# Cross-attention and a gated low-rank layer on one core: another order on TensorE, transfers of 64 partitions, wider matmuls for the sums of squares

## The reference

```python
x = x + _L0_xattn_ref(_layernorm(x), ctx, ctx)     # x, ctx: (8, 512, 2048) float32
x = x + _L0_ffn_ref(_layernorm(x), router_w, A, B)

def _L0_xattn_ref(q, k, v):                # B, C, N = 8, 512, 2048; 8 heads of 64 channels
    qh = softmax(q over the 64 channels of a head)
    kh = softmax(k over the 2048 positions)
    kvs = einsum('bnhd,bnhe->bhde', kh, vh)
    out = einsum('bnhd,bhde->bnhe', qh, kvs)

def _L0_ffn_ref(x, router_w, A, B):        # 4 experts of rank 16, the best 2 are used
    logits = flat @ router_w.T
    gates = softmax(logits where among the top 2, else -inf)
    mid = einsum('tf,erf->ter', flat, A)
    delta = einsum('te,teo->to', gates, einsum('ter,eor->teo', mid, B) * 4.0)
```

## Time and profile before

| | |
|---|---|
| median of 3 runs | 493.88 us (493.44 to 500.45) |
| the profiled execution | 496.45 us, of it 494.7 us from the first to the last instruction (the span) |
| PE busy | 416.6 us (84%) |
| DVE busy | 378.6 us (77%) |
| POOL busy | 358.8 us (73%) |
| ACT busy | 300.2 us (61%) |
| granted TensorE clock, mean | 0.92 |
| DMA | 137.99 MB, mean 279 GB/s |

### The profile page before, as it was taken

One profiled execution on the slowest core, in us unless ns is written; L12 is line 12 of the kernel. 1 busy time (PEld: TensorE's weight loads), 2 busy tenths in 40 slices (PEclk: granted clock), 3 DMA queues, 4 the chain that ended last, 5 costly groups with the idle time before them and its releaser, 6 DMA issues.

```text
span 494.7 us, 22911 instructions
## 1 busy us (share of the span) xinstructions
PE 416.6 (84%) x9960; PEld 362.5 (73%) x9960; DVE 378.6 (77%) x1045; ACT 300.2 (61%) x404; POOL 358.8 (73%) x341
## 2 busy tenths in 40 slices
PE   6659888988978887887988896898897878999975
PEld 6648777877867676776877675787776767788864
DVE  2488758896868967887897876868895978976864
ACT  1367767766648566574867665666674848586410
POOL 0459978987869767877797876867895987898510
PEclk9657978999989988999899997988998999999997
DMA  8997877899899888999899997899997998755347
GB/s 300 416 366 219 295 225 258 257 298 326 260 315 291 237 315 277 288 315 299 298 280 350 294 303 248 251 310 301 336 302 227 326 296 284 247 177 207 121 187 256
DMA packets 38996, 137.99 MB, mean 279 GB/s; under 512 B 4208, under 2 KB 6384, under 8 KB 38768
## 3 DMA queue, kind: packets, MB, share of 16 engines
q1 hardware_dynamic: 38896, 136.52, 82.3%
HBM read 102.95 MB, written 33.55 MB: 276 GB/s over the span
## 4 chain that ended last, share of the span: by engine, by line
PE 72%; issue 12%; DVE 7%; DMA 4%; SPq 3%; POOL 1%; ACT 1%; DVEq 0%; POOLq 0%
PE num_ps L404 17%; PE kv_ps L384 15%; PE raw_ps L421 13%; PE delta_ps L469 10%; PE kv_ps L436 7%; PE delta_ps L470 6%; DMA ctx_sb<-in_ctxt_dram 4%; DVE y_sb L705 2%; DVE attnT L696 2%; PE kv_ps L369 2%; SPq L234 1%; PE raw_ps L455 1%; PE num_ps L361 1%; DVE bn_parts L638 1%; SPq L229 1%
## 5 line engine op out<-in xcount | busy, mean ns | idle before, releaser
L322 POOL TENSOR_TENSOR y_sb<-attnT,y_sb 128x512 f32<-128x512 f32 x128 | 164.2, 1283 | 68.1 <-DVE attnT L696 67.4
L310 POOL TENSOR_TENSOR ek_sb<-ctx_sb,kmax_row 128x512 f32<-128x512 f32 x128 | 167.4, 1309 | 41.5 <-ACT kmax_row L502 40.8
L705 DVE TENSOR_TENSOR y_sb<-delta_ps,y_sb 128x512 f32<-128x512 f32 x128 | 87.4, 685 | 55.9 <-PE delta_ps L470 54.9
L404 PE MATMUL num_ps<-kv_sb,x_sb 64*64 64x65 f32 x4096 | 97.3, 233 | 18.4 <-issue 11.8
L384 PE MATMUL kv_ps<-ctx_sb,ek_sb 128*64 128x65 f32 x2048 | 100.3, 241 | 14.3 <-issue 14.0
L404 PEld LDWEIGHTS num_ps<-kv_sb,x_sb 64*64 64x64 f32 x4096 | 78.1, 142 | 34.2 <-issue 20.3
L384 PEld LDWEIGHTS kv_ps<-ctx_sb,ek_sb 128*64 128x64 f32 x2048 | 79.6, 146 | 28.4 <-issue 17.8
L421 PE MATMUL raw_ps<-w_sb,y_sb 128*64 128x69 f32 x2048 | 93.5, 232 | 6.8 <-issue 6.8
L621 DVE TENSOR_REDUCE max_n<-ctx_sb 128x32 f32<-128x512 f32 x128 | 86.4, 677 | 11.1 <-DMA ctx_sb<-in_ctxt_dram 11.1
L696 DVE TENSOR_TENSOR attnT<-num_ps,rden 128x512 f32<-128x512 f32 x128 | 88.5, 691 | 4.5
L469 PE MATMUL delta_ps<-midT,b_hi 128*128 128x256 f32 x256 | 84.2, 349 | 3.8 <-issue 3.1
(11 more groups left out here) (62 smaller groups left out, 423.6 us busy)
## 6 DMA issues: line engine op xcount, KB each, us to landing
ctx_sb<-in_ctxt_dram SPq DMA_DIRECT2D x64, 520.0 KB, 5.5
x_sb<-in_x_dram SPq DMA_DIRECT2D x64, 512.0 KB, 6.3
y_sb<-in_xt_dram SPq DMA_DIRECT2D x64, 512.0 KB, 6.5
out_dram<-y_sb SPq DMA_DIRECT2D x60, 512.0 KB, 6.0
out_dram<-y_sb SPq DMA_DIRECT2D x8, 256.0 KB, 3.6
sq_a<-in_bt_dram SPq DMA_DIRECT2D x1, 1024.0 KB, 15.8
w_sb<-in_wt_dram SPq DMA_DIRECT2D x1, 552.0 KB, 9.5
cst<-in_consts_dram SPq DMA_DIRECT2D x1, 145.0 KB, 2.4
```

The lines of the kernel that those rows point to most:

```text
L310: pool.tensor_tensor(ek_sb[:, t % 2, chunks(g), :].rearrange("p (a b) c -> p a b c", b=2), ctx_sb[:, t % 4, 2 * g:2 * g + 2, 1:P + 1, :].r ...
L322: pool.tensor_tensor(y, attnT[:, g, :], y, ALU.add).then_inc(x1_made, 1)
L404: mm = pe.matmul(num_ps[n, h, j * (DH + 1):(j + 1) * (DH + 1)], x_sb[d, t % 4, c * P + half * DH:c * P + (half + 1) * DH], kv_sb[d, t % 2, ...
L705: dve.tensor_tensor(y, delta_ps[i % 2][:].rearrange("p (j t c) -> p t j c", j=2, t=2), y, ALU.add).then_inc(out_made, 1)
```

## The change

TensorE keeps its operations but runs them in two orders. In even quarters: delta, turn_max, sum_squares, fold_squares, numerator, kv, project. In odd quarters: project, kv, spread_kmax, numerator, turn_mid, delta. DVE adds a delta one quarter later (`add_delta(*delta_at(q - 1))`).

The core of the diff:

```diff
-            STEP = 4 // PIECES
-            for q in range(0, 4 * NT + 28, STEP):
...
+            ctx_piece = x_piece = xt_piece = out_piece = (cst_landed, 16)
+            for q in range(0, 4 * NT + 28):
+                part = q % 2
+                p, r = divmod(q - part - 26, 8)
                 if 0 <= p < NP - 1:
...
+                    t, k = 2 * p + r // 2 % 2, r // 4
+                    sp.wait_ge(out_made, 8 * p + 4 * (k + 1))
+                    after(sp, *out_piece)
+                    store(t, k, part)
+                    out_piece = (out_stored[t % 8], 64 * (t // 8) + 32 * k + 16 * part + 16)
+                t, r = divmod(q - part + 10, 4)
                 if 3 <= t < NT:
-                    after(sp, num_done, 4 * (t - 4) + r + STEP)
-                    load_x(t, r // STEP)
+                    after(sp, num_done, 4 * (t - 4) + r + 2)
+                    after(sp, num_done, quarters_done(q, 5))
+                    after(sp, *x_piece)
+                    load_x(t, r // 2, part)
...
-                t, r = divmod(q + 16, 4)
-                if t < NT:
-                    sp.wait_ge(kv_done, 4 * (t - 4) + r + STEP)
-                    load_ctx(t, r // STEP)
+                t, r = divmod(q - part + 14, 4)
+                if 4 <= t < NT:
+                    sp.wait_ge(kv_done, 4 * (t - 4) + r + 2)
+                    after(sp, kv_done, quarters_done(q, 0))
+                    after(sp, *ctx_piece)
+                    load_ctx(t, r // 2, part)
...
-                for k in range(NCH // 4):
-                    for s in range(4):
-                        sq = sq_b if k >= 2 else sq_a[:, t % 2, :]
-                        at = (4 * k + s) % 8 * P
-                        mm = pe.matmul(kv_ps[(t + 1) % 2][32 * s:32 * s + 32, 2 * P:3 * P], ones[:, 0:32],
-                                       sq[:, at:at + P], start=(k == 0), stop=(k == 3), skip_group_check=True)
+                to = kv_ps[(t + 1) % 2]
+                for s in range(4):
+                    sq = sq_b[:] if s >= 2 else sq_a[:, t % 2, :]
+                    at = s % 2 * 3 * P
+                    pe.matmul(to[32 * s:32 * s + 32, P:4 * P], ones[:, 0:32], sq[:, at:at + 3 * P],
+                              start=True, stop=False, skip_group_check=True)
+                for s in range(4):
+                    sq = sq_b[:] if s >= 2 else sq_a[:, t % 2, :]
+                    at = (6 + s % 2) * P
+                    mm = pe.matmul(to[32 * s:32 * s + 32, P:2 * P], ones[:, 0:32], sq[:, at:at + P],
+                                   start=False, stop=True, skip_group_check=True)
...
-                pe.matmul(raw_ps[p % 2][:, odd, COL_SQ:COL_SQ + 2], sq_sum[:, t % 2, :], ones[:, 0:2],
-                          start=False, stop=True, skip_group_check=True).then_inc(sq_done, 1)
+                for k in range(3):
+                    mm = pe.matmul(raw_ps[p % 2][:, odd, COL_SQ:COL_SQ + 2], sq_sum[:, t % 2, k, :], ones[:, 0:2],
+                                   start=False, stop=(k == 2), skip_group_check=True)
+                mm.then_inc(sq_done, 1)
...
             for q in range(FIRST, LAST + 1):
-                delta(*delta_at(q))
-                turn_max(q)
-                sum_squares(q)
-                if q == 1:
-                    sum_w()
-                numerator(*tile_at(q, 5))
-                spread_kmax(q)
-                kv(*tile_at(q, 0))
-                project(*tile_at(q, 7))
-                fold_squares(q)
-                turn_mid(q)
+                if q % 2 == 0:
+                    delta(*delta_at(q))
+                    turn_max(q)
+                    sum_squares(q)
+                    fold_squares(q)
+                    numerator(*tile_at(q, 5))
+                    kv(*tile_at(q, 0))
+                    project(*tile_at(q, 7))
+                else:
+                    project(*tile_at(q, 7))
+                    kv(*tile_at(q, 0))
+                    spread_kmax(q)
+                    numerator(*tile_at(q, 5))
+                    turn_mid(q)
+                    if q == 1:
+                        sum_w()
+                    delta(*delta_at(q))
```

More of the change, by code:

```diff
@@ L221, in _, with rows, load_ctx, load_x @@
         def _(sp):
[L222 to L227, removed]
+            XW = N // 2
+            CP = NCH // 4
+            YC = NCH // 2
+            def rows(part):
+                return slice(part * DH, (part + 1) * DH)
+            def load_ctx(t, k, part):
                 c = slice(k * CP, (k + 1) * CP)
-                sp.dma_start(ctx_sb[:, t % 4, c, :, :].rearrange("p a c b -> p a (c b)"),
-                             ctxt[t][:, c, :, :].rearrange("p a c b -> p a (c b)")).then_inc(ctx_landed[t % 4], 16)
-            def load_x(t, k):
+                sp.dma_start(ctx_sb[rows(part), t % 4, c, :, :].rearrange("p a c b -> p a (c b)"),
+                             ctxt[t][rows(part), c, :, :].rearrange("p a c b -> p a (c b)")
+                             ).then_inc(ctx_landed[t % 4], 16)
+            def load_x(t, k, part):
                 c = slice(k * XW, (k + 1) * XW)
-                sp.dma_start(x_sb[:, t % 4, c], x_rows[t * P:(t + 1) * P, c]).then_inc(x_landed[t % 4], 16)
-            def load_y(t, k):
+                sp.dma_start(x_sb[rows(part), t % 4, c], x_rows[t * P + part * DH:t * P + (part + 1) * DH, c]
+                             ).then_inc(x_landed[t % 4], 16)
+            def load_y(t, k, part):
                 c = slice(k * YC, (k + 1) * YC)
-                sp.dma_start(y_sb[:, t % 8, c, :], xt[t][:, c, :]).then_inc(y_landed[t % 8], 16)
-            def store(t, k):
+                sp.dma_start(y_sb[rows(part), t % 8, c, :], xt[t][rows(part), c, :]).then_inc(y_landed[t % 8], 16)
+            def store(t, k, part):
                 c = slice(k * YC, (k + 1) * YC)
-                sp.dma_start(out[t, :, c, :].rearrange("p j c -> p (j c)"),
-                             y_sb[:, t % 8, c, :].rearrange("p j c -> p (j c)")).then_inc(out_stored[t % 8], 16)
+                sp.dma_start(out[t, rows(part), c, :].rearrange("p j c -> p (j c)"),
+                             y_sb[rows(part), t % 8, c, :].rearrange("p j c -> p (j c)")
+                             ).then_inc(out_stored[t % 8], 16)
             def store_last(i):
@@ L251, in whole @@
             def whole(load, t):
-                for k in range(PIECES):
-                    load(t, k)
+                for k in range(2):
+                    for part in range(2):
+                        load(t, k, part)
             def quarters_done(q, offset):
@@ L285, in _ @@
                 if 2 <= t < NT:
[L286 removed]
                     if t >= 8:
[L288 to L293 removed]
+                        sp.wait_ge(out_stored[t % 8], 64 * (t // 8))
+                    after(sp, *xt_piece)
@@ new lines, in _ @@
+                    load_y(t, r // 2, part)
+                    xt_piece = (y_landed[t % 8], 64 * (t // 8) + 16 * r + 16 * part + 16)
+                t, r = divmod(q - part + 14, 4)
[4 more added lines that the diff above has]
+                    load_ctx(t, r // 2, part)
+                    ctx_piece = (ctx_landed[t % 4], 64 * (t // 4) + 16 * r + 16 * part + 16)
@@ L559, in copy_squares @@
                 after(act, sq_done, t - 1)
-                act.activation(sq_sum[:, t % 2, :], kv_ps[(t + 1) % 2][:, 2 * P:3 * P], ACT.Copy,
+                act.activation(sq_sum[:, t % 2, :, :].rearrange("p k c -> p (k c)"), kv_ps[(t + 1) % 2][:, P:4 * P], ACT.Copy,
                                scale=1.0 / 32.0).then_inc(sq_summed, 1)
@@ L816, in _ @@
                 bn_part(*tile_at(q, -5))
[L817 removed]
+                add_delta(*delta_at(q - 1))
                 if a is not None:
```

22 lines of the change are left out of this document (8 added, 14 removed).

## The result

The changed kernel took 675.6 us (median of 4, 673.92 to 679.71) against 494.04 us: 1.370 times as long, 95% interval 1.364 to 1.376. I had forecast 464 us with a range of 447 to 530. A ratio with an interval rests on the faster executions of both kernels alone, since single executions of the kernel before spread from 484 to 507 us, and so it can differ by 1 or 2% from the quotient of the medians.

What follows compares the result with a forecast made beforehand. TensorE was taken as the bound, with late instruction fetches. Terms of -33 - 10 - 13 - 3 + 13 = -46 us gave 3.06 us a quarter; the transfer pace of 3.2 replaced it: 60.2 + 112 x 3.2 + 43 = 462, forecast 464, range 447 to 530.

Steps and rivals of the forecast that it cites:

- Step 1: PE's waits for late instruction fetches: fewer bytes in flight remove two thirds of them, -33 us.
- Step 2: TensorE's clock: two thirds of the time lost at the lower clock is won back, -10 us.
- Step 3: Deltas on TensorE: two side by side take 1.14 instead of 1.34 us, -13 us.
- step 7: Numerators at unequal distances: two deltas cover the division while DVE is on time; if late, PE waits; no size.
- Steps 4 and 5: Squares on TensorE: the fold saves starts, -3 us; sum_squares takes two more matmuls a tile, +13 us.
- Step 6: Fold ahead of the numerator on PE: it waits for ACT's squares, +10 us, parallel to the transfer pace.
- Step 8: Pace of transfers: a quarter can't be shorter than one 256 KB landing, taken as 3.1 us, 3.2 with issue.
- rival C: Slower: the landing of transfers becomes the bound; 519 us at 3.7 us a quarter; chance 0.19.
- rival D: Much slower: transfers of 64 partitions don't get the full rate; 550 to 710 us; chance 0.14.

Runs made afterwards that it cites:

- e8: Changed kernel with two pieces of each kind in flight instead of one, each half with its own semaphores: 575.93 us.
- e4: Kernel before with only the squares of the change (three chunks per matmul in fold_squares and sum_squares): 486.16 us, 0.982 of before.
- e12: Kernel before with the change's squares and 256 KB pieces by quarter columns over 128 partitions, no landing wait: 497.68 us, 1.016 of before.
- e11: Kernel before with both the new TensorE order and the squares of the change, transfers unchanged: 501.23 us, 1.008 of before.
- e7: Changed kernel with pieces of 128 partitions by a quarter of the columns and without the landing waits: 498.07 us.
- e3: Kernel before with only TensorE's opposite order in odd quarters and DVE's addition one quarter later: 501.63 us, 1.023 of before.
- e5: All computation left out, SP alone moves data in eleven stages: 403 GB/s for loads over 128 partitions, 206 GB/s over 64.
- e2: Changed kernel with its 256 KB pieces cut by columns over 128 partitions, still one of each kind in flight: 618.11 us, 1.247 of before.
- e1: Kernel before with each 512 KB piece sent as two transfers of 64 partitions back to back, no landing wait: 538.08 us against 496.39.
- e6: Changed kernel without the four waits for the piece before of the same kind, pieces of 64 partitions kept: 577.83 us.

## Why the prediction was wrong, point by point

**What bounds the kernel before: right in the main.** "Issue" is late instructions: in the trace of the kernel before all 32 such idle times of PE over 0.5 us end 1.2 to 1.6 us after a packet of the instruction queue has ended, and in e8 all 31 do so 1.2 to 1.7 us after one, while such packets are 5 to 7 us apart in the median. That data in flight make them late is borne out by e8 against the change, the same computation and bytes, differing in the number of pieces in flight. Of PE from 100 to 500 us (e8):

```profile
PE num_ps L425 <- issue: 27.2, 12, 4.8
PE kv_ps L405 <- issue: 13.5, 6, 3.7
PE delta_ps L497 <- DVE y_sb L742: 10.5, 17, 1.6
```

and of the changed kernel from 100 to 600 us:

```profile
PE delta_ps L490 <- DVE y_sb L732: 58.2, 12, 5.9
PE kv_ps L383 <- DVE kmax L658: 41.2, 12, 4.5
...
PE raw_ps L435 <- issue: 1.8, 1, 1.8
```

Over the whole span it is 62.9 against 4.0 us. The two differ in one thing more: PE waits 145.9 us for DVE in the changed kernel and 46.0 in e8, and in such a wait a late fetch goes unseen, so not all of the 59 us need be shorter fetches. The rule of the Trainium skill that such crossings are mostly hidden ("Runtime: NRT & Kernel Launch", section "Instruction fetch mechanics") agrees with the changed kernel (4.0 us), not with the one before (49.8 us).

**Step 1, fetch stalls: right in direction.** Nearly all went, not two thirds, but in a kernel in which PE was no longer the bound, so it was worth nothing and the size stays unproven. Where PE still leads the chain, pieces of half the bytes took issue waits from 37.7 (e4) to 20.5 us (e12), and in the new order only from 37.4 (e11) to 34.5 (e7).

**Step 2, clock: wrong sign.** The issue waits went, and longer waits for data came: a mean granted clock of 0.92 became 0.776.

**Step 3, deltas side by side: the size right, the value wrong.** In the changed kernel two deltas take 308.51 to 309.66 us, 1.15 us as worked out:

```profile
308.51 0.39 PE L490 MATMUL delta_ps<-midT,b_hi 128*128 128x256 f32 x1
...
309.66 0.52 PE L450 MATMUL kv_ps<-sq_a,cst 128*32 128x384 f32 x2
```

But with PE as the bound (e3) the order gains nothing. I had the reason in step 7, DVE late, and gave it no price.

**Steps 4 and 5: sizes right within 0.08 us, the sum's sign wrong.** +10 us was forecast, e4 measured -1.8%; why is open.

**Step 6: right.** The fold waits 7.4 us for ACT in e3, where 10 were put.

**Step 8, the pace: this is the step that failed.** I saw the mechanism, a quarter not shorter than one landing, and bounded the landing at 2.8 to 4.2 us, then took 3.1 because "the rule itself holds back the traffic"; it measured 4.2 to 4.6. The rule does not hold traffic back here: when landings set the pace, nearly four pieces are always in flight, since each kind issues 0.1 us after its landing. The value for three others in flight belonged there, 4.0 to 4.2 us at 128 partitions (e5, e2), which is my upper bound. I also wrote that a piece of 256 KB was not in the trace. One was, in the page of the kernel before:

```profile
out_dram<-y_sb SPq DMA_DIRECT2D x8, 256.0 KB, 3.6
```

These are the last stores, over 128 partitions, issued some 0.9 us apart, so with about four in flight. With their 3.6 us the sum is 519 us, which is rival C and no longer "no change or faster". With 4.2 us, and 0.1 us to issue, my own sum gives 60 + 112 x 4.3 + 43 + 2, about 587 us; e2, the case for it, took 618, with 4.38 us a quarter and an end 15 us longer than I had. The rest is the half rate of 64 partitions, which lifts the landing to 4.2 to 4.6 us here and costs at the start (+17 us, in e1 and e6 as well). I had left it as rival D with 0.14, and its range of 550 to 710 us holds the result; that is partly luck, as it put on the partitions alone what the wait does for the larger part. e2 and e6 put 120 us on the wait and 80 on the partitions when each comes alone.

The miss adds up: the first 112 steps took 4.61 us and not 3.2, +158 us; the last 15 took 3.46 and not 2.85, +9; the start +17, the end +28. 464 and these 212 are 676 us. Two smaller slips of mine change nothing: C at 3.6 us a quarter gives 508 and not 506 us, and the middle of D is 630.

**Not in the sum at all:** the end. 120 stores one after the other were counted at the pace of the loop, but the last 15 come when no other work spreads them: +28 us. It is the wait again, lengthened by the partitions: the end is 25.0 us before the change, 26.6 in e6 without the wait, 39.9 in e2 with it over 128 partitions, 53.4 in the change.

**The probabilities.** C and D were exclusive rivals in my text, but they are two factors on one term. Both had reasons in the text and none against them but "buffers even out single late pieces", which says nothing on a late mean.

## What to carry to other kernels

Look in the page of the old kernel for any transfer of the new size before drawing a line between others. Before limiting transfers in flight, compare the landing under that very load, all kinds in flight, with the time in which the kernel consumes a piece: bytes in flight over landing time is the rate, and 4 x 256 KB over 4.0 to 4.9 us is 260 to 215 GB/s, where this kernel moves up to 303. Cut pieces by columns or by whole tiles, not by partitions, and check the pattern alone with a stage of transfers without computation. A shorter stall is worth something only on the engine that is still the bound after the change.

## What the runs showed of the hardware that I had not expected

Loads and stores mixed, with the two halves issued back to back, reach 276 to 282 GB/s (e1), well over the 236 GB/s of alternating loads alone. And in e5 quarter columns without waits run at 348 GB/s against 403 for half columns over the same 128 partitions; rows (2 and 4 KB) and pieces (256 and 512 KB) are both halved there, so which of them costs isn't shown. In the kernel it cost nothing that could be seen (e7, 498 us).
